# A macaron layer on one core: a fourth buffer behind the experts, chunk 3's norm moved into attention, and the prologue in another order

## The chip, the core and the metric

The kernel runs on one core of one Trainium2 chip. The core has five engines with queues of their own: PE (TensorE, matrix products), DVE (VectorE), ACT (ScalarE), POOL (GpSimd) and SP (SyncE, which only issues transfers here). They run side by side, wait for each other by semaphores, and share the on-chip memory and the eight accumulator banks that PE writes. The metric is the time of one execution on the device in microseconds (us).

## The reference

The input is x with 2 × 1024 tokens of width 128. Five steps are added to it one after the other:

```python
x = x + 0.5 * ffn0(layernorm(x))      # 16 experts, the best 4 of each token
x = x + ssm(layernorm(x))             # a convolution with powers of a, gelu, projection, layernorm
x = x + 0.5 * ffn0(layernorm(x))      # the same experts again
x = x + 0.5 * ffn1(layernorm(x))      # a dense product plus low-rank experts, the best 2 of 10
x = x + attention(layernorm(x))       # 16 heads of width 8, keys and values through a latent of 32
x = x + 0.5 * ffn1(layernorm(x))
```

An expert of ffn0 computes `glu = gate * sigmoid(1.702 * gate)`, `act = (clip(up) + 1) * glu` and `act @ down`, weighted by the token's share for that expert; the shares are a softmax over the four largest of 16 logits. In the ssm step the convolution's kernel holds the powers of a per-channel number, `a ** t` for t = 0 to 1023.

## The kernel before

The 2048 tokens are cut into four chunks of 512 (`CH`, `NC`). All float32 products are made of three products of parts: each operand is split into a high part, which the matrix unit takes in one pass, and a low part, and `split_matmul` (lines 1815 to 1817) adds high×high, low×high and high×low. So nearly every product needs two helpers: ACT copies the high part, DVE or POOL subtracts it to get the low part.

**The expert loop.** Both passes of ffn0 make one loop of `JOBS` = 128 slots (2 passes × 4 chunks × 16 experts). In a slot PE runs `expert_halves` of the slot's expert (gate and up, six products), `expert_score` in the first slots (line 1949, the shares spread over all partitions), and `expert_down` of the expert three slots earlier (lines 1966, 1967 and 1969; the last of them takes the low part). DVE runs `expert_up` (line 1344), `expert_act` of the expert before (line 1366) and `expert_weighted` (line 1355); ACT runs `expert_glu` (line 996, the gelu) and `expert_hi` (line 1010), POOL `expert_lo` (line 810). Results of these steps lie in rings: `act`, and its high and low parts in `act_parts`, have three places each (`NACT`).

Between the slots lie side chains: "in" brings a chunk in, normalizes it and makes its shares; "ssm" is the ssm step and the way to the second pass; "last" is the norm and ffn1 of chunks 0 to 2. Two tables say at which slot a step of a chain is issued on an engine: `BASE` has the slot at which a chunk's chain begins, and `STEPS` the distance of a step from it. Negative slots are the prologue, in which chunks 0 and 1 come in. `SINGLE` has the steps that occur once: `split_small` (router weights and vectors), `split0` to `split3` (the experts' weights, four experts at a time; ACT line 918 and DVE line 1331) and `powers` (lines 1319 to 1323: four small operations and a scan over 1023 elements, which the ssm step of chunk 0 needs). At each slot an engine runs its expert steps and then the side steps of that slot, in the order of the program.

**Attention.** Behind the loop, queries, keys and values of batch 0 (chunks 0 and 1) are made. Their high and low parts are put on top of each other by transfers that SP issues (`stack`, line 662), in four groups of heads; group 0 has sixteen transfers of its own, four for each of q0, k0, q1 and k1. A bound on the scores (`maxima`, line 1471, `top_norms`, `attn_bound` on PE, `root_of_bound` on POOL, `attn_spread` on PE, line 2099) gives `minus_c`, which ACT adds in the exponentials. Then 256 units run: PE makes a unit's scores (line 2111), DVE corrects those near the diagonal (`fix_scores`, line 1660), ACT takes exponentials (line 1084), and PE multiplies them into the values (line 2143). A step t of PE is two units. The tables `FIRST` and `EARLY` put other work between the units, by t for PE and by unit for DVE and ACT: what is left of ffn1 (z, weights, back), the norms and queries of batch 1, and the last ffn1 of chunks 0 to 2. Chunk 3's norm ahead of ffn1 (`LN_FFN1A`: transposes on PE, statistics on DVE, the norm on POOL, rows on ACT, transposes back at line 1863, high part at line 948, low part at line 1214) stands ahead of the first unit. The ffn1 of chunk 3 closes the program.

## Time and profile before

| | us |
|---|---|
| median of 3 runs | 710.6 (708.65 to 711.17) |
| the profiled execution, own time | 711.55 |
| its span on the core | 709.0 |
| busy: PE / ACT / DVE / POOL | 612.3 / 536.1 / 500.3 / 284.7 |

An engine's busy time is the time in which at least one of its instructions ran; its matrix products overlap, so their lengths add up to more. "Idle before" in a row is the time for which the engine had nothing to run just before that row's instructions, and the name behind the arrow is what ended most of it. The span falls into a prologue (to about 30 us), the expert loop (to about 392), attention (to about 674) and the last ffn1 of chunk 3. PE is the busiest engine in the loop and ACT in attention.

### The profile page before, as it was taken

What the parts mean: (1) busy time and instruction counts of PE and PEld (TensorE: products, weight loads), DVE (VectorE), ACT (ScalarE), POOL (GpSimd) and SP (SyncE); (2) the same over time, 40 slices, a digit from 0 to 9 for tenths busy, and PEclk for the clock granted to TensorE, in tenths of its full rate; (3) what the DMA queues carried; (4) which work ended last, traced back from release to release, by engine and by line L of the source; (5) the groups of instructions that cost most, each with busy time, mean ns of one, the idle gap of its engine ahead of it and who ended that gap; (6) DMA issues with size and microseconds to landing.
All of it is one profiled execution on the core that took longest, in us unless ns stands there. A gap on an engine that the chain in (4) does not pass through costs nothing.

```text
span 709.0 us, 11201 instructions
## 1 busy us (share of the span) xinstructions
PE 612.3 (86%) x3623; PEld 358.2 (51%) x3623; DVE 500.3 (71%) x1290; ACT 536.1 (76%) x735; POOL 284.7 (40%) x307
## 2 busy tenths in 40 slices
PE   2798898979989999999998589998987999999835
PEld 1575676657766677767676333333322333333213
DVE  3889888879988899899889634457552576555422
ACT  4566566675867857767556599999999999999911
POOL 3277557676676767555564601123310010000000
PEclk9999999999999999999999779999999999999965
DMA  9100332333333333334331699000049900000000
GB/s 263 39 1 1 125 101 90 100 79 105 91 95 100 91 95 102 104 98 127 112 98 30 147 191 244 14 0 2 1 83 196 187 13 1 1 15 16 16 3 15
DMA packets 32382, 56.64 MB, mean 80 GB/s; under 512 B 4752, under 2 KB 13424, under 8 KB 30944
## 3 DMA queue, kind: packets, MB, share of 16 engines
q1 hardware_dynamic: 31136, 55.48, 30.3%
q8 instruction: 30, 0.49, 0.3%
q0 software_dynamic: 224, 0.34, 0.2%
q14 instruction: 32, 0.26, 0.1%
q10 hardware_dynamic: 960, 0.07, 0.1%
HBM read 35.72 MB, written 3.38 MB: 55 GB/s over the span
## 4 chain that ended last, share of the span: by engine, by line
PE 30%; issue 19%; ACT 19%; DVE 15%; POOL 14%; DMA 1%; ACTq 1%; POOLq 0%; DVEq 0%
ACT raw_w L1084 13%; POOL act_parts L810 9%; PE bank L2143 8%; PE bank L1815 4%; PE bank L2111 4%; PE bank L1817 3%; DVE act L1366 3%; PE bank L1816 3%; DVE bank L1355 2%; DVE up L1344 2%; POOL rstd L757 2%; DVE stats L1204 2%; PE bank L1969 1%; DMA vecs<-in_vecs 1%; ACT L996 1%
## 5 line engine op out<-in xcount | busy, mean ns | idle before, releaser
L1084 ACT ACTIVATE raw_w<-bank,minus_c 128x1024 f32<-128x1024 f32 x256 | 260.1, 1148 | 4.1 <-PE bank L2111 3.4
L810 POOL TENSOR_TENSOR act_parts<-act,act_parts 128x512 fp32r<-128x512 f32 x128 | 167.9, 1315 | 104.3 <-ACT act_parts L1010 102.6
L1010 ACT ACTIVATE act_parts<-act 128x512 fp32r<-128x512 f32 x128 | 80.7, 631 | 97.4 <-DVE act L1366 97.1
L1660 DVE TENSOR_TENSOR bank<-bank,fix 128x256 f32<-128x256 f32 x128 | 55.5, 434 | 99.8 <-PE bank L2111 99.6
L1815 PE MATMUL bank<-xn_parts,w_hi 128*128 128x512 f32 x256 | 109.1, 426 | 13.8 <-DVE up L1344 9.9
L1344 DVE TENSOR_SCALAR up<-bank,b_up 128x512 f32<-128x512 f32 x128 | 95.3, 744 | 24.1 <-PE bank L1817 21.8
L1817 PE MATMUL bank<-xn_parts,w_hi 128*128 128x512 f32 x256 | 101.2, 395 | 0.0
L1816 PE MATMUL bank<-xn_parts,w_lo 128*128 128x512 f32 x256 | 100.8, 394 | 0.0
L1366 DVE SCALAR_TENSOR_TENSOR act<-up,bank 128x512 f32<-128x512 f32 x128 | 86.7, 677 | 0.0
L996 ACT ACTIVATE bank<-bank,b_gate 128x512 f32<-128x512 f32 x112 | 73.0, 652 | 10.4 <-PE bank L1817 10.1
L754 POOL TENSOR_SCALAR var_eps<-mean_var 128x4 f32<-128x4 f32 x28 | 6.4, 228 | 179.7 <-DVE mean_var L1535 117.0
L2143 PE MATMUL bank<-raw_w 128*9 128x512 f32 x512 | 68.4, 607 | 10.4 <-ACT raw_w L1084 9.5
L2143 PE MATMUL bank<-raw_w,act 128*9 128x512 f32 x512 | 66.9, 595 | 9.8 <-ACT raw_w L1084 9.3
L1815 PEld LDWEIGHTS bank<-xn_parts,w_hi 128*128 128x128 f32 x256 | 48.4, 189 | 36.6 <-DVE up L1344 21.2
L1969 PE MATMUL bank<-act_parts,w_hi 128*128 128x512 f32 x128 | 52.1, 407 | 9.1 <-POOL act_parts L810 9.0
L1817 PEld LDWEIGHTS bank<-xn_parts,w_hi 128*128 128x128 f32 x256 | 48.3, 189 | 11.2
L1816 PEld LDWEIGHTS bank<-xn_parts,w_lo 128*128 128x128 f32 x256 | 48.6, 190 | 7.5
L1966 PE MATMUL bank<-act_parts,w_hi 128*128 128x512 f32 x128 | 51.4, 402 | 0.0
L1967 PE MATMUL bank<-act_parts,w_lo 128*128 128x512 f32 x128 | 50.6, 395 | 0.0
L930 ACT ACTIVATE xt<-bank,offset,rstd 128x128 f32<-128x128 f32 x76 | 28.5, 461 | 13.6 <-POOL offset L763 13.6
L1355 DVE SCALAR_TENSOR_TENSOR bank<-bank,grow 128x512 f32<-128x512 f32 x48 | 33.2, 693 | 4.3 <-ACT bank L996 4.3
L1969 PEld LDWEIGHTS bank<-act_parts,w_hi 128*128 128x128 f32 x128 | 24.0, 188 | 20.9 <-POOL act_parts L810 15.7
(251 smaller groups left out, 980.1 us busy)
## 6 DMA issues: line engine op xcount, KB each, us to landing
grow<-scores SPq DMA_DIRECT2D x48, 256.0 KB, 3.2
early<-scores SPq DMA_DIRECT2D x32, 256.0 KB, 3.2
raw_w<-scores SPq DMA_DIRECT2D x32, 256.0 KB, 3.2
raw_w<-in_gate_up SPq DMA_DIRECT2D x4, 512.0 KB, 7.3
w_lo<-gelu_parts SPq DMA_DIRECT2D x8, 256.0 KB, 5.3
w_lo<-act_parts SPq DMA_DIRECT2D x8, 256.0 KB, 5.6
w_hi<-gelu_parts SPq DMA_DIRECT2D x6, 256.0 KB, 4.7
w_hi<-act_parts SPq DMA_DIRECT2D x6, 256.0 KB, 5.6
```

The lines of the kernel that those rows point to most:

```text
L810: pool.tensor_tensor(act_lo[:, j % NACT, :], act[:, j % NACT, :], act_hi[:, j % NACT, :].bitcast(F32), ALU.subtract).then_inc(s["lo_ready" ...
L996: eng.activation(out, bank[:, gate_bank(j), :], ACT.Gelu_apprx_sigmoid, bias=b_gate[:, e:e + 1]).then_inc(s["glu_ready"], 1)
L1010: eng.activation(act_hi[:, j % NACT, :], act[:, j % NACT, :], ACT.Copy).then_inc(s["hi_ready"], 1)
L1084: eng.activation(probs[:, u % NP, :], pair, ACT.Exp, bias=minus_c[:, b:b + 1])\
L1344: eng.tensor_scalar(up[:, j % 2, :], bank[:, up_bank(j), :], b_up1[:, e:e + 1], 1.0 - LIMIT, ALU.add, ALU.max).then_inc(s["up_ready"], 1)
L1366: eng.scalar_tensor_tensor(out=act[:, j % NACT, :], in0=up[:, j % 2, :], scalar=1.0 + LIMIT, in1=bank[:, weighted_bank(j), :], op0=ALU.min ...
L1660: eng.tensor_tensor(pair, pair, turned, ALU.mult).then_inc(s["fixed"], 1)
L1815: pe.matmul(out, w_hi, v_hi, start=start, stop=False)
L1816: pe.matmul(out, w_lo, v_hi, start=False, stop=False)
L1817: return pe.matmul(out, w_hi, v_lo, start=False, stop=stop)
L1969: last = pe.matmul(out, w0_hi[:, e, 2, :], act_lo[:, slot, :], start=False, stop=e == E0 - 1)
L2143: last = pe.matmul(bank[32 * j:32 * j + VW, O_BANK, :], values[b][:, kb, HG * g + j, :], probs[:, u % NP, CH * (j % 2):CH * (j % 2 + 1)], ...
```

## The change

It has three parts.

1. **A fourth buffer.** The rings of high and low parts get a place more (`NDOWN` = 4), `act` keeps three. `expert_down` now takes the expert four slots earlier, the loop runs one slot longer, `add_out` and the chains "ssm" and "last" move by one slot or stay. The memory for it comes from five small weights, which now lie in `resid`, and from `fix` and `minus_one`, which now lie in `tmp`: `fix` is loaded within the loop behind the last use of `tmp`, and POOL writes `minus_one` behind its low parts of the keys.
2. **The prologue.** Chunk 0's chain begins at slot −16 (−13 before) and the split of the small weights at −12 (−9), so that chunk 0's shares and scores stand ahead of the first weight split on DVE and of chunk 1's logits on PE. The scan of powers is cut into two halves of 511 and 512 elements, at slots −10 and −5 (one scan at slot 13 before).
3. **Chunk 3's norm inside attention.** ACT copies the transposed tokens (`keep_tokens`), DVE's statistics come behind q1's low part, POOL's norm behind the bound, and rows, high and low part are made by DVE at units 3, 5 and 6; PE transposes back at t = 2. z of chunk 2 comes ahead of that, the logits of chunk 3 behind. q1's stack transfers of group 0 come last, with a semaphore of their own that PE waits for at t = 8. DVE makes one half of k1's low part (`last_key_lo`), POOL the other, and DVE's maxima stand ahead of q1's low part.

```diff
-BASE = {"in": (-13, -12, 0, 11), "ssm": (20, 35, 51, 67), "last": (83, 99, 115)}
+BASE = {"in": (-16, -12, 0, 11), "ssm": (20, 36, 52, 68), "last": (84, 100, 116)}
...
-    "act": {"split_small": -9, "split0": -7, "split1": -3, "split2": 0, "split3": 2, "split_squares": 11, "mix0": 24, "mix1": 26, "mix2": 28},
-    "dve": {"split_small": -9, "split0": -6, "split1": -2, "powers": 13, "mix2": 29},
+    "act": {"split_small": -12, "split0": -9, "split1": -3, "split2": 0, "split3": 2, "split_squares": 11, "mix0": 24, "mix1": 26, "mix2": 28},
+    "dve": {"split_small": -12, "powers0": -10, "split0": -6, "powers1": -5, "split1": -2, "mix2": 29},
...
-    "pe": {0: ("logits", 3, 0), 1: ("logits", 3, 1), 3: ("z", 2, None), 5: ("weights", 2, None), 7: ("scores", 3, None),
+    "pe": {0: ("z", 2, None), 2: ("t2", 3, None), 3: ("logits", 3, 0), 4: ("logits", 3, 1), 5: ("weights", 2, None),
+           8: ("scores", 3, None), 9: ("back", 2, 0), 10: ("back", 2, 1), 13: ("a_t1", 2, None), 15: ("z", 3, None), 17: ("weights", 3, None),
...
-        NACT = 3
+        NACT, NDOWN = 3, 4
...
-        w_down = sb("w_down", [D, LAT])
+        w_up = resid[0:LAT, 0, 0:2 * D].rearrange("l (i d) -> l i d", i=2)
...
+            first_queries(0)
+            first_keys(0)
+            first_keys(1)
+            first_queries(1)
...
             query_lo(0)
             key_lo(0)
-            key_lo(1)
-            norm(LN_FFN1A, NC - 1)
+            key_lo(1, 0)
+
+            pool.memset(minus_one, -1.0)
...
             root_of_bound(0)
+            norm(LN_FFN1A, NC - 1)
...
+            def keep_tokens(n, c):
+                k = norm_at(n, c)
+                eng.wait_ge(s["t1_ready"], nth_t1(n, c))
+                eng.wait_ge(s["t2_ready"], k - 1)
+                eng.activation(xt[:, k % 2], bank[:, t1_bank(n, c), :].rearrange("p (t d) -> p t d", d=D), ACT.Copy)\
+                   .then_inc(s["t1_copied"], 1)
...
+            def last_key_lo():
+                c, i = QC - 1, 1
+                eng.wait_ge(s["v_ready"], c + 1)
+                eng.wait_ge(s["k_hi_ready"], 2 * c + i + 1)
+                eng.wait_ge(s["k_lo_ready"], 2 * c)
+                eng.tensor_tensor(xn_parts[:, i, chunk(c)], k_f[c][:, i, :], k_hi[:, i, place(c)].bitcast(F32),
+                                  ALU.subtract).then_inc(s["k_lo_ready"], 1)
...
-                norm_stats(LN_FFN1A, NC - 1)
-                query_lo(1)
                 maxima(0)
                 maxima(1)
                 top_norms(0)
+                last_key_lo()
                 take_bound(0)
-                norm_lo(LN_FFN1A, NC - 1)
+                query_lo(1)
+                first_stats(LN_FFN1A, NC - 1)
...
-            for slot in range(FIRST_SLOT, JOBS + 3):
+            for slot in range(FIRST_SLOT, JOBS + 4):
...
-                e, c, slot = j % E0, j // E0 % NC, j % NACT
+                e, c, slot = j % E0, j // E0 % NC, j % NDOWN
...
+                if t == KB:
+                    pe.wait_ge(s["stack0_late"], 16 * SLOTS)
...
                 keys(1)
+                norms(0)
                 values_in(1)
                 norm_in(LN_FFN1A, NC - 1, X_FFN0B)
-                norms(0)
                 norms(1)
                 pe.wait_ge(s["v_copied"], QC)
                 attn_bound(0)
-                norm_out(LN_FFN1A, NC - 1)
+                attn_spread(0)
                 pe.wait_ge(s["maxes_ready"], QC)
-                pe.wait_ge(s["xn_ready"], nth_hi(LN_FFN1A, NC - 1))
+                pe.wait_ge(s["t1_copied"], 1)
                 score_pair(0)
-                attn_spread(0)
...
-                if slot >= 3:
-                    expert_down(slot - 3)
+                if slot >= 4:
+                    expert_down(slot - 4)
```

How the rows of an engine move, at three places. First DVE in the prologue, from chunk 0's low part (L1214) on; L1228 to L1252 is the pick of a chunk, L1263 to L1299 are its shares, L1331 a weight split. Before:

```order
L1214 TENSOR_TENSOR xn_parts<-bank,xn_parts 128x512
L1228 TENSOR_TENSOR logit<-bank,router_b 128x4x16
L1233 TENSOR_TENSOR logit<-logit,bank 128x4x16
L1238 MAX top<-logit 128x8 x4
L1249 MATCH_REPLACE taken<-top,logit 128x20 x4
L1252 TENSOR_TENSOR shifted<-logit,top 128x64
L1214 TENSOR_TENSOR xn_parts<-bank,xn_parts 128x512
L1331 TENSOR_TENSOR w_lo<-raw_w,w_hi 128x1536
L1228 TENSOR_TENSOR logit<-bank,router_b 128x4x16
L1233 TENSOR_TENSOR logit<-logit,bank 128x4x16
L1238 MAX top<-logit 128x8 x4
```

After (the powers are L1320 to L1328):

```order
L1214 TENSOR_TENSOR xn_parts<-bank,xn_parts 128x512
L1320 TENSOR_SCALAR ab<-ab 128x1
L1321 RECIPROCAL ab<-ab 128x1
L1322 TENSOR_TENSOR ab<-vecs 128x1
L1323 TENSOR_SCALAR ab<-vecs 128x1
L1328 SCALAR_TENSOR_TENSOR early<-ab,zero 128x511
L1228 TENSOR_TENSOR logit<-bank,router_b 128x4x16
L1233 TENSOR_TENSOR logit<-logit,bank 128x4x16
L1238 MAX top<-logit 128x8 x4
L1249 MATCH_REPLACE taken<-top,logit 128x20 x4
L1252 TENSOR_TENSOR shifted<-logit,top 128x64
L1263 SCALAR_TENSOR_TENSOR picked<-taken,expd 128x64
```

The shares of chunk 0 stood behind the low part of chunk 1, a weight split and chunk 1's pick; now they stand directly behind its own pick, and the powers stand ahead of that pick.

Second, PE where the down projections begin: L1815 to L1817 are gate or up of an expert, L1949 its score, L1963 and L1964 the bias, L1966 to L1969 expert 0's down projection. Before:

```order
L1815 MATMUL bank<-xn_parts,w_hi 128x512 [waits up_ready]
L1816 MATMUL bank<-xn_parts,w_lo 128x512
L1817 MATMUL bank<-xn_parts,w_hi 128x512
L1949 MATMUL bank<-score_t,sel 128x512 [waits act_ready]
L1963 MATMUL bank<-score_t,db_hi 128x512 [waits score_ready]
L1964 MATMUL bank<-score_t,db_lo 128x512
L1966 MATMUL bank<-act_parts,w_hi 128x512 [waits hi_ready]
L1967 MATMUL bank<-act_parts,w_lo 128x512
L1969 MATMUL bank<-act_parts,w_hi 128x512 [waits lo_ready]
```

After (the same lines are L1827 to L1829, L1961, L1975 and L1976, and L1978 to L1981):

```order
L1827 MATMUL bank<-xn_parts,w_hi 128x512 [waits glu_ready,w0_lo_ready]
L1828 MATMUL bank<-xn_parts,w_lo 128x512
L1829 MATMUL bank<-xn_parts,w_hi 128x512
L1827 MATMUL bank<-xn_parts,w_hi 128x512 [waits up_ready]
L1828 MATMUL bank<-xn_parts,w_lo 128x512
L1829 MATMUL bank<-xn_parts,w_hi 128x512
L1961 MATMUL bank<-score_t,sel 128x512 [waits act_ready]
L1975 MATMUL bank<-score_t,db_hi 128x512 [waits score_ready]
L1976 MATMUL bank<-score_t,db_lo 128x512
L1978 MATMUL bank<-act_parts,w_hi 128x512 [waits hi_ready]
L1979 MATMUL bank<-act_parts,w_lo 128x512
L1981 MATMUL bank<-act_parts,w_hi 128x512 [waits lo_ready]
```

The down projection of an expert has moved behind the gate and up products of one more expert.

Third, PE at the start of attention: L1847 are the transposes of chunk 3, L2067 and L2068 sums of squares by head, L2094 the bound, L1863 the transposes back, L2111 the first score pair, L2099 the spread of the bound. Before:

```order
L1847 MATMUL bank<-ident,x 128x128 [waits normalized,x_ready]
L1847 MATMUL bank<-ident,x 128x128 x3
L2067 MATMUL bank<-score_t,same_head 128x512 [waits q_decayed,k_decayed,k_sq_ready,q_sq_ready]
L2068 MATMUL bank<-score_t,same_head 128x512
L2067 MATMUL bank<-score_t,same_head 128x512 [waits q_decayed,k_decayed,k_sq_ready,q_sq_ready]
L2068 MATMUL bank<-score_t,same_head 128x512
L2094 MATMUL bank<-ident,tops 1x128 [waits tops_ready,v_copied]
L1863 MATMUL bank<-ident,xt 128x128 [waits xn_ready,normalized]
L1863 MATMUL bank<-ident,xt 128x128 x3
L2111 MATMUL bank<-w_hi 128x512 [waits stack0_loaded,xn_ready,maxes_ready]
L2111 MATMUL bank<-w_hi 128x512 x3
L2099 MATMUL bank<-bound,minus_one 128x1 [waits sqrt_ready]
```

After (the transposes are L1859, the sums L2079 and L2080, the bound L2106, its spread L2111, the score pair L2123, and z of chunk 2 L1827 to L1829):

```order
L1859 MATMUL bank<-ident,x 128x128 [waits normalized,x_ready]
L1859 MATMUL bank<-ident,x 128x128 x3
L2079 MATMUL bank<-score_t,same_head 128x512 [waits q_decayed,k_decayed,k_sq_ready,q_sq_ready]
L2080 MATMUL bank<-score_t,same_head 128x512
L2106 MATMUL bank<-ident,tops 1x128 [waits tops_ready,v_copied]
L2111 MATMUL bank<-bound,tmp 128x1 [waits sqrt_ready]
L2123 MATMUL bank<-w_hi 128x512 [waits stack0_loaded,t1_copied,maxes_ready]
L2123 MATMUL bank<-w_hi 128x512 x3
L1827 MATMUL bank<-xn_parts,sq_hi 128x512 [waits z_copied,minus_c_ready]
L1828 MATMUL bank<-xn_parts,sq_lo 128x512
L1829 MATMUL bank<-xn_parts,sq_hi 128x512
```

The transposes back are gone from the place ahead of the first score pair, and the spread of the bound has come ahead of it.

## Rows read from the trace of the kernel before

**Rows 1.** Page, groups: line, operands, count; busy us, mean ns; idle before.

```profile
L1084 ACT ACTIVATE raw_w<-bank,minus_c 128x1024 f32<-128x1024 f32 x256 | 260.1, 1148 | 4.1 <-PE bank L2111 3.4
```

**Rows 2.** Waits of PE, 40 to 392 us: waiter, releaser; total us, times, longest.

```profile
PE bank L1815 <- DVE up L1344: 9.9, 16, 1.7
PE bank L1969 <- POOL act_parts L810: 9.0, 12, 1.3
```

**Rows 3.** Waits of DVE, same stretch.

```profile
DVE up L1344 <- PE bank L1817: 20.7, 26, 1.7
DVE bank L1355 <- ACT bank L996: 11.8, 8, 3.8
```

**Rows 4.** Timeline, prologue: start us, length us, engine, line, operation, [idle before, releaser].

```profile
20.63 0.22 DVE L1252 TENSOR_TENSOR shifted<-logit,top 128x64 f32<-128x64 f32 x1
...
25.13 0.22 DVE L1263 SCALAR_TENSOR_TENSOR picked<-taken,expd 128x64 f32<-128x64 f32 x1
...
21.50 0.40 PE L1879 MATMUL bank<-r_split,xn_parts 128*128 128x32 f32 x1 [1.53 <-DVE xn_parts L1214]
...
26.53 0.67 PE L1895 MATMUL bank<-ident,share_hl 128*32 128x128 f32 x4 [0.37 <-DVE share_hl L1299]
...
29.88 0.50 PE L1815 MATMUL bank<-xn_parts,w_hi 128*128 128x512 f32 x1 [0.64 <-ACT glu L996]
...
25.41 1.47 ACT L918 ACTIVATE w_hi<-raw_w 128x1536 fp32r<-128x1536 f32 x1
...
27.24 0.59 ACT L985 ACTIVATE score_t<-bank 32x512 fp32r<-32x512 f32 x1 [0.36 <-PE bank L1895]
...
27.84 1.28 ACT L996 ACT_TABLE_LOAD   x1
...
29.14 0.69 ACT L996 ACTIVATE glu<-bank,b_gate 128x512 f32<-128x512 f32 x1
```

**Rows 5.** Timeline around the powers (DVE, PE); another scan's line, min/median/max ns.

```profile
66.68 0.15 DVE L1319 TENSOR_SCALAR ab<-ab 128x1 f32<-128x1 f32 x1
...
68.01 3.16 DVE L1323 TENSOR_TENSOR_SCAN early<-ab,zero 128x1023 f32<-128x1023 f32 x1
...
71.86 0.50 PE L1815 MATMUL bank<-xn_parts,w_hi 128*128 128x512 f32 x1 [1.61 <-DVE up L1344]
...
L1394 DVE TENSOR_TENSOR_SCAN raw_w<-raw_w,zero x4: 1212/1244/1276, 106.5 to 238.5; 128x512 f32<-128x512 f32 x4
```

**Rows 6.** Timeline, start of attention: DVE, POOL, PE, ACT.

```profile
396.67 2.33 DVE L1467 TENSOR_TENSOR act_parts<-glu,gelu_parts 128x512 fp32r<-128x512 f32 x2
...
398.93 2.47 DVE L1471 TENSOR_REDUCE head_max<-bank 128x1 f32<-128x512 f32 x4
...
407.28 0.43 DVE L1660 TENSOR_TENSOR bank<-bank,fix 128x256 f32<-128x256 f32 x1 [0.97 <-PE bank L2111]
...
394.21 2.53 POOL L844 TENSOR_TENSOR xn_parts<-up,early 128x512 fp32r<-128x512 f32 x2
...
396.70 3.43 POOL L844 TENSOR_TENSOR xn_parts<-resid,early 128x512 fp32r<-128x512 f32 x2
...
406.40 0.80 PE L2111 MATMUL bank<-w_hi 32*128 32x512 f32 x4 [1.46 <-DVE xn_parts L1214]
...
407.61 1.28 ACT L1084 ACT_TABLE_LOAD   x1
```

**Rows 7.** SP's DMA issues there; table of issues: KB each, us to landing.

```profile
399.49 1.26 SPq L662 DMA_DIRECT2D w_hi<-act_parts  x2
...
402.09 1.26 SPq L662 DMA_DIRECT2D w_hi<-xn_parts  x2
...
w_hi<-xn_parts SPq DMA_DIRECT2D x4, 128.0 KB, 2.7
```

**Rows 8.** Stretches: length, busy us by engine, granted PE clock, DMA share, GB/s.

```profile
407.60:420.00 12.40, 10.87 (x65) 4.23 (x65) 4.45 (x24) 10.69 (x11) 0.00 (x0) 0.67 0.98 196
420.00:434.00 14.00, 13.00 (x102) 4.49 (x102) 5.80 (x13) 13.78 (x15) 2.78 (x2) 1.00 0.99 190
```

159 lines of the change are left out of this document (75 added, 84 removed).

## The prediction, made before the changed kernel was timed

> **What bounds the kernel now.** The profiled execution took 711.55 us, 2.55 us of it outside its span of 709.0; the median of the runs shown is 710.6, so the sum below, made against 711.55, is about 1 us high against the median. A measurement of this kernel can tell about 0.5% (3.6 us) from no change; the three chances at the end go by that.
>
> I read the page's groups first. In attention ACT is the bound: 256 exponentials of 1.148 us keep it busy for 260.1 us and only 4.1 us of idle stand ahead of them [rows 1]. So whatever lets the first exponential start earlier moves the end by as much, unless PE can't feed it. In the expert loop PE is the bound, with gaps. The waits of PE from 40 to 392 us show two large ones: 9.0 us in 12 for L1969, the third matmul of a down projection, released by POOL's low part (L810), and 9.9 us in 16 for L1815, released by DVE's `up` (L1344) [rows 2]. The waits of DVE in that stretch show that it has air, 20.7 us in 26 behind PE, and 11.8 us in 8 behind ACT's gelu [rows 3]. So a PE wait on POOL is mostly a true loss, but where ACT is the late one, removing it only moves the wait. Last I read three timelines, of the prologue, of the powers and of the start of attention; they carry the terms below.
>
> **Prologue.** Before, chunk 0's `pick` on DVE ends at 20.85 (20.63 + 0.22), but its shares start only at 25.13, behind the low part of chunk 1, the first weight split and chunk 1's pick: 4.28 us [rows 4]. Now they follow directly, so chunk 0's scores on PE move from 26.53 [rows 4] to about 22.2. That alone brings no expert forward, because two other things move back. PE's logits(1) started at 21.50; they now stand behind scores(0) and behind ACT's copy of them: 22.2 + 0.67 + 0.59 (the lengths of the two in [rows 4]) = 23.5, which is 2.0 us later. DVE's pick(1), ACT's exp(1) and ACT's second weight split behind it move with them. ACT: split 25.41 + 2.0 = 27.4, its 1.47 gives 28.9, the table load 1.28 gives 30.2 and the first gelu 0.69 gives 30.9, against 29.14 + 0.69 = 29.83 before; before, ACT had the copy of the scores between split and table load, and now has not, which is why 2.0 becomes 1.1. PE's halves(1) waited for that gelu (29.88) and will again [rows 4]. DVE's own queue grows by the powers: the four small operations and half of the scan. A 512-wide scan of another line takes 1.244 us at the median; half of the 3.16 us one would be 1.58 [rows 5]. DVE has about as much idle while it waits for logits, so this hides at the first place and adds at most 0.7 at the second. The split of small weights moves ahead of other work on ACT and DVE, but it waits for a transfer of vectors either way; I give it nothing, at most 0.4 us of gain. **+1.1 us (0 to +1.8).**
>
> **Expert loop, the fourth buffer.** PE's down(slot−3) becomes down(slot−4). POOL's low part then has one slot more, about 2.8 us (128 experts from 29.9 [rows 4] to 392, the end of the stretch of [rows 2]), and the longest wait for it was 1.3 us [rows 2]. So all 9.0 us of this wait should go. What is late next? On PE the next thing is gate and up of the following expert, which wait for DVE's `up` and ACT's gelu. DVE's waits are 20.7 behind PE against 11.8 behind ACT [rows 3]; where DVE waits behind PE a PE gain passes on, where it waits for ACT the gain is given back. So I count 20.7 / (20.7 + 11.8) = 0.64 of 9.0, that is 5.8 us. The extremes are 9.0 (all of it) and about 3 (DVE takes over at most places). The side chains move by one slot (20, 36, 52, 68 for 20, 35, 51, 67), which changes what they collide with but adds no instruction. At the end one more down projection stands behind the last halves: three matmuls, at most 3 × 0.50 = 1.5 us by the length of one in [rows 5]; I count 0.2, near the lower end, since attention waits there for other engines' work, not for PE's [rows 6].
>
> **Expert loop, the powers.** Five DVE operations between 66.68 and 71.17 (68.01 + 3.16) leave the loop, 4.4 us of DVE in one slot. PE's visible wait behind them is 1.61 us at 71.86 [rows 5]; DVE then runs the slots back to back until it has caught up, so part of the 9.9 us in [rows 2] that follows is theirs too. Between 1.6 and 4.4 I take 2.2, near the wait that is shown. The price in the prologue is counted above. **Loop together: −5.8 −2.2 +0.2 = −7.8 us (−4 to −12).**
>
> **Start of attention.** Before, PE's first score pair at 406.40 waited 1.46 us for DVE's low part of chunk 3's norm [rows 6], the end of a chain through POOL, ACT, PE, ACT and DVE. minus_c came behind that pair, then ACT loaded its table (407.61, 1.28 us) and the first exponential followed at 408.90 [rows 6]. Now the chain of the norm lies inside attention. Left ahead of the first pair are two chains. (a) The bound: the maxima (before at 398.93, after the statistics and q's low part, 2.33 us [rows 6]) start at the latest where that low part started, 396.67, and end 2.47 us later at 399.1; tops, transpose, root and spread follow. With the 1.28 us of table load behind them they may take 3.9 us before this chain and not the stacks sets the first exponential (404.3, below, less 1.28, less 399.1); before, all of that but the spread lay within the 5.0 us between the maxima's end at 401.4 and the pair at 406.40, with the norm's work in the same queues. I take it to be the earlier chain. (b) The stacks: SP issues about one DMA per 0.65 us (two in 1.26 us) and each lands 2.7 us after its issue [rows 7]. The last of group 0 was the second of the pair at 402.09; with q1's four sent last, k1's low part takes the place of the pair at 399.49, if its data are there. That data is now made by DVE (last_key_lo) at about 398.5 to 399.2. So: 399.49 + 0.63 + 2.7 = 402.8, and the first pair can run at about 403.0, 3.4 us earlier. Fix of the first pair ended at 407.28 + 0.43 = 407.71 [rows 6], 1.31 after the pair's start, so the first exponential comes at 403.0 + 1.3 = 404.3 against 408.90: −4.6. In front of the first exponentials PE now has z(2) and t2(3) in place of logits, at a granted clock of 0.67 (the level of 1.2 GHz for part of the time) [rows 8], where PE was 10.87 of 12.40 us busy; I take 0.6 back. **−4.0 us (−1.5 to −5.5).**
>
> last_key_lo is a two-input DVE operation that now stands beside POOL's same work on the other half. In the trace, POOL's two L844 took 2.53 us with DVE elsewhere and 3.43 beside DVE's L1467, whose two took 2.33 [rows 6]: about 0.45 us for each. By that row the low part is done in time for its slot in SP's queue. The Trainium skill, "SBUF — State Buffer", section "SBUF: two separate sides", says more: DVE and GpSimd share a port pair under an exclusive lock, and whichever starts first holds it for the whole instruction while the other "fully blocks". By that, one whole POOL operation would stand ahead of last_key_lo, and the term would be about −3.2 for −4.0; the rows show the partial price, and I keep to them.
>
> Attention proper is ACT's pitch, so the end moves with the first exponentials. Nothing is changed in the tail.
>
> **Sum.** +1.1 −7.8 −4.0 = −10.7: 711.55 − 10.7 = 700.85, and from the median 710.6 − 10.7 = 699.9. I predict 700.5.
>
> **Rivals.**
> R1, the low parts' wait turns into a wait for DVE's `up`: for it speaks that this wait is already the larger one [rows 2]; against it DVE's 20.7 us of waits behind PE [rows 3]. The loop then gives −3.3 for −7.8, and the time is 705.
> R2, the first pair doesn't come forward, because the last stack isn't earlier or t2 and z on one bank hold PE: attention gives −1.5 for −4.0: 703. R1 and R2 together: 707.5.
> R3, slower: the granted clock stays at 0.67 through the side chains of the first half of attention, because PE waits in order for z_copy, t_rows and hi where it had logits before. It is 0.67 until 420.0 now, after a stretch in which PE did little but wait (the last of it the 1.46 us at 406.40 [rows 6]); then 1.00, and PE is busy for 13.00 us of 14.00 [rows 8]. At half of that clock such a stretch holds 26 us of PE work in 14, so each further us at the low level costs up to 0.86 us. It decides from 12.4 us on (to about 432), when it eats the whole 10.7; with 17 us it ends at 714.5. Against it: ACT was 10.69 of 12.40 us busy in the low stretch too [rows 8], so PE fed it. The Trainium skill, page "TensorE: Matmul & The Clock Gate", section "A second HAM failure mode: psum-queue depth-cycling", reports such an oscillation from short idles between groups of matmuls; the trace shows none after 420.
> R4, the change doesn't do what it says: shares come early but no expert does. That is my forecast for the prologue already.
>
> **How the numbers follow.** Forecast 0.55 (696.5 to 704); R1 0.17 (705); R2 0.12 (703); both 0.10 (707.5); R3 0.06 (714.5). Faster by over 0.5% means below 707.0: the forecast, R1 and R2 but for some spread, 0.84; within 0.5% is R1 and R2 together and a little of the rest, 0.12; slower 0.04. The bounds of the terms added up give 694 to 707.5; with all extremes at once unlikely at the fast side, the range is 694.5 to 707.5.
>
> **What would show it.** After: no wait of PE on POOL's low part above 0.2 us in the loop, PE's wait for `up` at the old powers gone, halves(1) near 31 us, scores(0) near 22; the first exponential 4 to 5 us nearer to the loop's end, its pair released by the stack transfer; granted clock back at 1.00 within some 11 us of it. I am wrong if PE's waits for `up` grow by more than 4 us (R1), if the first pair still waits for something other than the stacks (R2), or if the low clock lasts past unit 16 (R3).

## The result and the profile after

The changed kernel took 700.41 us (median of 5 runs, 698.8 to 700.93) against 710.6 beside it (708.65 to 712.8): the ratio is 0.9843, with a 95% interval of 0.9816 to 0.987. The forecast was 700.5. The profiled execution took 698.8 us, with a span of 696.3. Two more series of the same kernel gave 0.9842 and 0.9827.

The span of a trace can be cut at four events that both kernels have: the start of the split of the small weights on ACT (which begins the routing of chunk 0), the gate product of expert 1 on PE, the loop's last add on DVE, and the first exponential. Worked out from the timelines, in us:

| | small weights start | to expert 1 | to the last add | to the first exponential | to the end of the span | span |
|---|---|---|---|---|---|---|
| before | 13.82 | 16.06 | 361.79 | 17.23 | 300.10 | 709.0 |
| after | 11.19 | 17.89 | 353.21 | 13.72 | 300.29 | 696.3 |
| difference | −2.63 | +1.83 | −8.58 | −3.51 | +0.19 | −12.7 |
| forecast | 0 | +1.1 | −7.8 | −4.6 | +0.6 | −10.7 |

**The prologue.** ACT, PE and the table of DMA issues (the last number is the time from issue to landing), to compare with [rows 4]:

```profile
11.19 0.23 ACT L903 ACTIVATE r_split<-raw_r 128x32 fp32r<-128x32 f32 x1
...
26.68 1.28 ACT L997 ACT_TABLE_LOAD   x1
27.98 0.69 ACT L997 ACTIVATE glu<-bank,b_gate 128x512 f32<-128x512 f32 x1
...
19.51 1.04 PE L1907 MATMUL bank<-ident,share_hl 128*32 128x128 f32 x4 [0.41 <-DVE share_hl L1299]
21.31 0.37 PE L1891 MATMUL bank<-r_split,xn_parts 128*128 128x32 f32 x1 [0.77 <-ACT score_t L986]
...
29.08 0.78 PE L1827 MATMUL bank<-xn_parts,w_hi 128*128 128x512 f32 x1
...
vecs<-in_vecs ACTq DMA_DIRECT2D x1, 4.0 KB, 6.3
```

Scores(0) on PE (L1907) come at 19.51 and logits(1) (L1891) behind them at 21.31, with ACT's copy between; split, table load and gelu follow in the forecast order, and expert 1 starts at 29.08 instead of 29.88. But the work from the small weights on begins 2.63 us earlier than before, since their split was not held up by the transfer of the vectors: it landed 6.3 us after its issue, 8.8 before. Counted from that start the new order is 1.83 us slower. Of that the gelu has 1.47 (16.79 us behind the start, 15.32 before). And expert 1 does not wait for the gelu any more, which ended at 28.67: its row names no wait, and the chain of work that ended last runs through DVE's second half of the powers, chunk 1's shares and PE's queue:

```profile
24.93 1.27 DVE early L1328
...
27.10 1.05 PE bank L1907 x4
```

PE was still at its lower clock there: these four products took 1.05 us where the same four took 0.60 before, and those of expert 1 are mostly 0.63 us long where they had been 0.40.

**The loop.** Waits of PE and then of DVE in the stretch of [rows 2, 3] (total us, times, longest):

```profile
PE bank L1827 <- DVE up L1345: 7.5, 14, 1.7
PE bank L1827 <- issue: 4.0, 3, 1.3
PE bank L1827 <- DVE sq_lo L1799: 2.4, 1, 2.4
```

```profile
DVE up L1345 <- PE bank L1829: 15.5, 21, 1.5
DVE bank L1356 <- ACT bank L997: 10.1, 8, 2.6
```

The wait for POOL's low part, 9.0 us in 12, is gone. The wait for DVE's `up` has not grown but fallen, from 9.9 to 7.5; it contained what the powers had cost. Two waits have grown in their place, both at the ssm step's projections: 2.4 for `sq_lo` and 4.0 in three under "issue". In the kernel before the two rows of that view for the same places are:

```profile
PE bank L1815 <- issue: 2.2, 3, 0.8
...
PE bank L1815 <- DVE sq_lo L1787: 1.2, 1, 1.2
```

DVE has less air, 15.5 us behind PE for 20.7.

One thing is new. Two stretches around the first projection, with the granted clock as the third number from the end; behind them the first of them in the kernel before, and then PE's timeline of the changed kernel at its start:

```profile
110.00:117.00 7.00, 4.89 (x17) 3.92 (x18) 5.22 (x9) 3.59 (x7) 4.05 (x4) 0.76 0.28 75
117.00:130.00 13.00, 13.00 (x60) 9.87 (x59) 12.10 (x27) 8.35 (x16) 9.36 (x10) 1.00 0.32 102
```

```profile
110.00:117.00 7.00, 5.07 (x20) 3.40 (x19) 4.31 (x8) 6.53 (x10) 5.92 (x6) 1.00 0.28 76
```

```profile
112.11 0.47 PE L1827 MATMUL bank<-gelu_parts,sq_hi 128*128 128x512 f32 x1 [2.43 <-DVE sq_lo L1799]
...
112.89 0.39 PE L1827 MATMUL bank<-xn_parts,w_hi 128*128 128x512 f32 x1
113.12 0.40 PE L1828 MATMUL bank<-xn_parts,w_lo 128*128 128x512 f32 x1
113.35 0.57 PE L1829 MATMUL bank<-xn_parts,w_hi 128*128 128x512 f32 x1
113.72 0.63 PE L1827 MATMUL bank<-xn_parts,w_hi 128*128 128x512 f32 x1
114.15 0.63 PE L1828 MATMUL bank<-xn_parts,w_lo 128*128 128x512 f32 x1
```

PE waits 2.43 us, and 1.2 us after it has started again its matmuls are 0.63 us long for 0.40, at a pitch of 0.43 for 0.23: the clock has gone from 2.4 to 1.2 GHz for some 3.4 us (0.76 over 7 us). In the trace of before all of the loop stood at 1.00; its first projection came at 116.73, behind a wait of 1.24 us.

What the fall cost can be read from two runs described below, which wait 2.44 us at the same place without a fall (the powers in the loop, and the old prologue). From DVE's `up` of slot 30 to that of slot 36, first in the changed kernel, then with the powers in the loop:

```profile
111.88 0.74 DVE L1345 TENSOR_SCALAR up<-bank,b_up 128x512 f32<-128x512 f32 x1
...
127.37 0.75 DVE L1345 TENSOR_SCALAR up<-bank,b_up 128x512 f32<-128x512 f32 x1
```

```profile
114.06 0.74 DVE L1339 TENSOR_SCALAR up<-bank,b_up 128x512 f32<-128x512 f32 x1
...
128.29 0.75 DVE L1339 TENSOR_SCALAR up<-bank,b_up 128x512 f32<-128x512 f32 x1
```

That is 15.49 us against 14.23 (14.23 with the old prologue too), so the fall costs 1.26 us.

**The start of attention.** To compare with [rows 6, 7]:

```profile
391.29 0.58 PE L2111 MATMUL bank<-bound,tmp 1*128 1x1 f32 x2 [2.10 <-POOL bound L853]
393.84 0.80 PE L2123 MATMUL bank<-w_hi 32*128 32x512 f32 x4 [1.97 <-DMA w_hi<-xn_parts]
...
391.91 0.17 ACT L1090 ACTIVATE minus_c<-bank 128x1 f32<-128x1 f32 x1 [2.61 <-PE bank L2111]
394.71 1.28 ACT L1078 ACT_TABLE_LOAD   x1 [2.63 <-PE bank L2123]
396.01 4.13 ACT L1078 ACTIVATE raw_w<-bank,minus_c 128x1024 f32<-128x1024 f32 x4
...
389.52 1.27 DVE L1466 TENSOR_TENSOR act_parts<-glu,gelu_parts 128x512 fp32r<-128x512 f32 x2
...
389.68 1.56 POOL L853 TENSOR_TENSOR bound<-bound,half_one 1x1 f32<-1x1 f32 x1 [0.96 <-DVE bound L1653]
...
390.11 1.26 SPq L651 DMA_DIRECT2D w_hi<-xn_parts  x2
```

The first score pair (L2123) waits for the stacks' transfer and nothing else, as forecast; it comes 11.55 us behind the last add (382.29) where it had been 14.73 behind it. But the table load, which I had expected to be over by then, starts only at 394.71, behind the wait for PE, and takes its 1.28 us in front of the exponential as before. The profile page's group of the exponentials is unchanged in size (259.9 us busy for 260.1, 4.9 us of idle for 4.1 in [rows 1]).

### The profile page after: what moved, and what is told of

It is laid out like the page before. It is cut to its first block, busy times and chain, and to the rows that moved or that the text cites. A ratio compares the mean times of both kernels' runs of the same rounds, so it can differ in the third digit from the quotient of the medians.

```text
span 696.3 us, 11204 instructions
## 1 busy us (share of the span) xinstructions
PE 612.3 (88%) x3623; PEld 362.0 (52%) x3623; DVE 500.7 (72%) x1297; ACT 533.0 (77%) x731; POOL 281.8 (40%) x306
## 4 chain that ended last, share of the span: by engine, by line
PE 41%; ACT 21%; DVE 20%; issue 13%; DMA 1%; POOL 1%; ACTq 1%; SPq 1%; DVEq 0%; POOLq 0%
ACT raw_w L1078 13%; PE bank L2157 8%; PE bank L1827 6%; PE bank L1829 5%; PE bank L1828 5%; DVE act L1365 5%; PE bank L2123 4%; DVE up L1345 3%; DVE bank L1356 3%; PE bank L1978 2%; PE bank L1979 2%; PE bank L1981 2%; ACT L997 2%; ACT bank L997 1%; DVE stats L1204 1%
## 5 line engine op out<-in xcount | busy, mean ns | idle before, releaser
L1078 ACT ACTIVATE raw_w<-bank,minus_c 128x1024 f32<-128x1024 f32 x256 | 259.9, 1144 | 4.9 <-PE bank L2123 4.2
L1672 DVE TENSOR_TENSOR bank<-bank,tmp 128x256 f32<-128x256 f32 x128 | 55.5, 434 | 98.3 <-PE bank L2123 98.1
L1827 PE MATMUL bank<-xn_parts,w_hi 128*128 128x512 f32 x256 | 109.9, 429 | 11.5 <-DVE up L1345 7.5
L1829 PE MATMUL bank<-xn_parts,w_hi 128*128 128x512 f32 x256 | 101.9, 398 | 0.0
L1827 PEld LDWEIGHTS bank<-xn_parts,w_hi 128*128 128x128 f32 x256 | 48.9, 191 | 35.1 <-DVE up L1345 18.4
L1829 PEld LDWEIGHTS bank<-xn_parts,w_hi 128*128 128x128 f32 x256 | 48.8, 190 | 11.2
L1978 PE MATMUL bank<-act_parts,w_hi 128*128 128x512 f32 x128 | 51.7, 404 | 0.0
L1981 PE MATMUL bank<-act_parts,w_hi 128*128 128x512 f32 x128 | 50.7, 396 | 0.0
L1356 DVE SCALAR_TENSOR_TENSOR bank<-bank,grow 128x512 f32<-128x512 f32 x48 | 33.2, 692 | 6.2 <-ACT bank L997 6.2
L931 ACT ACTIVATE xt<-bank,offset,rstd 128x128 f32<-128x128 f32 x72 | 27.0, 460 | 9.1 <-POOL offset L761 9.1
L755 POOL TENSOR_TENSOR rstd<-var_eps,half_pow 128x4 f32<-128x4 f32 x28 | 29.0, 1037 | 2.3
```

What stands on the lines that cost most here:

```text
L1078: eng.activation(probs[:, u % NP, :], pair, ACT.Exp, bias=minus_c[:, b:b + 1])\
L1827: pe.matmul(out, w_hi, v_hi, start=start, stop=False)
L1829: return pe.matmul(out, w_hi, v_lo, start=False, stop=stop)
L1978: pe.matmul(out, w0_hi[:, e, 2, :], act_hi[:, slot, :], start=False, stop=False)
```

## Experiments

All differences of stages below are between profiled executions and refer to the changed kernel's row in the table above; ratios are against the kernel before, timed beside each run.

| | ratio, 95% interval | small weights start | to expert 1 | to the last add | to the first exponential | to the end |
|---|---|---|---|---|---|---|
| three buffers | 0.9953 (0.9933 to 0.9973) | 14.21 | 17.88 | 360.31 | 13.67 | 302.43 |
| old prologue | 0.9863 (0.9817 to 0.9908) | 13.12 | 16.43 | 355.83 | 13.58 | 300.44 |
| powers in the loop | 0.9916 (0.989 to 0.9942) | 11.03 | 17.47 | 355.10 | 13.62 | 299.88 |
| old attention start | 0.9887 (0.9843 to 0.9931) | 11.06 | 17.53 | 353.38 | 17.33 | 301.10 |
| changed, again | 0.9842 (0.982 to 0.9864) | 11.04 | 17.88 | 352.97 | 13.76 | 300.15 |
| changed, third time | 0.9827 (0.9797 to 0.9857) | 11.03 | 17.88 | 353.21 | 13.71 | 301.27 |
| table load and stacks | 0.9814 (0.9788 to 0.984) | 12.29 | 17.89 | 353.11 | 11.89 | 299.52 |
| the same again | 0.9775 (0.9745 to 0.9806) | 11.79 | 17.88 | 352.97 | 11.95 | 299.71 |
| router weights first | 0.9841 (0.9817 to 0.9865) | 11.03 | 17.77 | 352.81 | 13.86 | 300.43 |
| projection later | 0.9903 (0.9873 to 0.9933) | 11.02 | 17.87 | 354.69 | 13.67 | 302.15 |
| mixed weights earlier | 0.984 (0.9811 to 0.9869) | 11.04 | 17.86 | 352.45 | 13.59 | 300.36 |
| the last and the first of these | 0.9808 (0.9767 to 0.985) | 11.31 | 17.89 | 352.45 | 11.97 | 302.68 |

### The fourth buffer taken away

```diff
-        NACT, NDOWN = 3, 4
+        NACT, NDOWN = 3, 3
...
-                if slot >= 4:
-                    expert_down(slot - 4)
+                if slot >= 3:
+                    expert_down(slot - 3)
```

> The changed kernel with the ring of parts back at three places, the down projection back at three slots behind and the chains ssm and last back at 20, 35, 51, 67 and 83, 99, 115; prologue and attention stay changed. Theory (the fourth buffer removes PE's wait for POOL's low part): PE waits for POOL in the third matmul of the down projection come back with 7 to 10 us, the last add of the loop comes 5 to 8 us later than in the changed kernel (382.3), the time is about 706 (704 to 708.5). Rival (the loop's gain is the powers' and the waits only change their name): the PE waits on POOL come back but the time is within 2 us of the changed kernel's 700.4.

708.27 us, 8.2 us above 0.9843 of the 711.28 measured beside it. PE's waits in that kernel, 40 to 392 us:

```profile
PE bank L1981 <- POOL act_parts L808: 8.7, 12, 1.2
PE bank L1827 <- DVE up L1345: 8.3, 15, 1.7
```

POOL's wait is back with 8.7 us in 12, and the loop is 7.10 us longer. The remaining 1.1 is no part of the loop in this trace, where attention took 2.1 us longer than in the changed kernel and the granted clock was once below 1.00 (0.83 over 540 to 550 us); but the profiled execution, 711.38 us, was the longest of ten, so it does not settle where the median has the 1.1. So the buffer is worth 7.1 of the loop's 8.6 us; by the 8.7 us of wait that it takes away, a share of 0.8 reached the end. The 7.1 are a net: the changed kernel loses 1.26 us to the fall of the clock at its first projection, which this run does not have, and from DVE's last `up` to the last add it took 5.4 us, as in the kernel before, for 5.9 with four buffers.

### The prologue and the powers put back

Two runs: the whole prologue as before with the powers at slot 13 (the diff, with ACT's splits back at −9 and −7 too), and the powers alone at slot 13, with chunk 0's chain and the small weights' split left at −16 and −12. The scan is one of 1023 elements again in both.

```diff
-BASE = {"in": (-16, -12, 0, 11), "ssm": (20, 36, 52, 68), "last": (84, 100, 116)}
+BASE = {"in": (-13, -12, 0, 11), "ssm": (20, 36, 52, 68), "last": (84, 100, 116)}
...
-    "dve": {"split_small": -12, "powers0": -10, "split0": -6, "powers1": -5, "split1": -2, "mix2": 29},
+    "dve": {"split_small": -9, "split0": -6, "split1": -2, "powers": 13, "mix2": 29},
```

> The changed kernel with the prologue of the kernel before: chunk 0's chain at -13, the split of the small weights at -9, the first weight split at -7 on ACT, and the powers as one scan at slot 13. Theory of the prediction (the reordered prologue costs 1.1 us and the powers out of the loop give 2.2): +1.1, about 701.5; the gate and up products of expert 1 start 1.1 us earlier than 29.1 in the changed kernel, that is near 28. Rival (the reordering itself brings the first experts forward by about 1 us, as the traces of before and after show 29.9 and 29.1): they start near 30 and the time is +3, about 703.5. Second rival (that 0.8 us is only the vectors' transfer landing earlier by chance): the start follows the landing of vecs in this run, 1.0 us per 2.6 us of landing.

> The changed kernel with only the powers moved back: one scan over 1023 elements at slot 13 in the loop, the rest of the changed prologue stays. Theory (powers in the loop cost 2.2 us, in the prologue at most 0.7): +1.5 to +2.2, about 702.3; a PE wait for DVE's up of 1 to 2 us appears near 70 us. Rival (all 4.4 us of DVE are on the path): +4. Second rival (in the prologue they cost as much as in the loop): 0.

The old prologue gave 701.44 us, near the 701.5 expected, but the interval of its ratio takes in the changed kernel's 0.9843. Counted from the small weights' start expert 1 comes after 16.43 us, 1.46 earlier than in the changed kernel, and the loop is 2.62 us longer. The row on PE's wait for `up` behind the scan:

```profile
71.58 0.79 PE L1821 MATMUL bank<-xn_parts,w_hi 128*128 128x512 f32 x1 [2.89 <-DVE up L1339]
```

The powers alone gave a prologue shorter by 0.42 and a loop longer by 1.89 us, with the same wait at the same place:

```profile
70.49 0.50 PE L1821 MATMUL bank<-xn_parts,w_hi 128*128 128x512 f32 x1 [2.87 <-DVE up L1339]
```

So by these traces the powers cost about 1.9 us in the loop and at most 0.4 in the prologue. Most of the 0.4 is the clock's: the run with the old start of attention, next, has the changed kernel's prologue with the powers in it, but expert 1's products were at the higher clock there (0.40 us long), waited 0.33 us for the gelu and came after 17.53 us, which leaves 0.06 us to the powers. The 1.9 are a net of two effects. At their own place the powers cost 3.05 us: from DVE's `up` of slot 12 to that of slot 16 it is 13.06 us with the powers alone in the loop and 10.01 in the changed kernel. Of that 1.26 are given back at the first projection, where the changed kernel's clock falls and this one's does not. The new order of shares, logits and splits costs the other 1.0 us of the prologue (1.46 less 0.42). The two runs differ by 0.73 us in the loop, and that is the clock's: both reach the `up` of slot 12 33.2 us behind expert 1, and from there to slot 16 the old prologue takes 13.77 for 13.06, with the clock down around that wait (0.66 over 70 to 75 us) in its trace alone. The old prologue's split of the small weights began when the vectors had landed, at 13.12. The run of the powers alone is odd in its times: its median, 704.02, is 4.2 us above its profiled execution (699.77, the shortest of nine), and its runs spread over 7.5 us. The two longest (707.32 and 706.85) had a mean granted clock of 0.959 and 0.961, the shortest 0.970; where they lost it the one trace doesn't show, and this stays open. By the ratio this run is 5.3 us above the changed kernel's repeat, which is nearer to the rival (all 4.4 us of DVE on the path) than to the theory's +1.5 to +2.2; against the rival speak the stages of this trace and the old prologue's run, which has the powers in the loop too and lies 1.5 us above the repeat.

### Attention's start put back

```diff
-            def first_queries(c):
+            for c in range(QC):
...
-            first_queries(0)
-            first_keys(0)
-            first_keys(1)
-            first_queries(1)
...
-                first_stats(LN_FFN1A, NC - 1)
+                norm_lo(LN_FFN1A, NC - 1)
...
-                pe.wait_ge(s["t1_copied"], 1)
+                norm_out(LN_FFN1A, NC - 1)
+                pe.wait_ge(s["xn_ready"], nth_hi(LN_FFN1A, NC - 1))
                 score_pair(0)
```

> The changed kernel with attention's start of the kernel before: chunk 3's norm ahead of the first unit, stacks in the order q0, k0, q1, k1, the maxima behind q's low part, all of k1's low part on POOL. Theory: the first exponential comes 17.2 us behind the last add of the loop again (408.90 - 391.67; 13.7 in the changed kernel) and the time rises by 3.3 to 4.0, to about 704. Rival (the norm inside attention holds PE at its lower clock and gives the gain back later): the first exponential is later by as much but the time rises by less than 1.5.

All of the third part of the change is undone here, the tables with it. 702.69 us; the ratio is 0.0045 above that of the changed kernel's repeat, which is 3.2 us. PE and ACT at the start of attention:

```profile
396.81 0.80 PE L2097 MATMUL bank<-w_hi 32*128 32x512 f32 x4 [1.46 <-DVE xn_parts L1201]
...
398.01 1.28 ACT L1071 ACT_TABLE_LOAD   x1
399.30 3.12 ACT L1071 ACTIVATE raw_w<-bank,minus_c 128x1024 f32<-128x1024 f32 x3
```

PE waits 1.46 us for the norm's low part, exactly as in [rows 6], and the first exponential is 17.33 us behind the last add: +3.61. The end moved by as much or more (attention behind it took 0.8 us longer), so nothing of the gain is given back and the lower clock is no price here.

### The transfer of the vectors

```diff
             def split_small():
-                eng.wait_ge(s["small_loaded"], 16 * len(SMALL))
+                eng.wait_ge(s["router_loaded"], 16 * 3)
...
+            def split_rest():
+                eng.wait_ge(s["small_loaded"], 16 * (len(SMALL) - 3))
```

> The changed kernel unchanged, as the control for the runs beside it. Expected 700.4 (698.5 to 703 for single runs). If the landing of the vectors' transfer, which was 10.6 to 14.2 us in the six profiles so far, sets the prologue, gate and up of expert 1 start 17.5 to 17.9 us behind the start of the small weights' split in this profile too (landing 11.2 or earlier: at 28.5 to 29.1).

> The changed kernel with the split of the small weights cut in two: the router's part waits for its own three transfers alone, the rest (down bias, vectors, up bias) follows behind chunk 0's high and low part. Theory (the landing of vecs sets when the prologue runs and gives most of the spread between runs): the router's split starts at about 11.1 us in any case, expert 1's products at 28.5 to 29.2, the median falls by about 1 us against the control and the spread of the runs shrinks from some 5 us to some 3. Rival (other transfers or the granted clock make the spread): median and spread are the control's.

> The changed kernel once more, as the control beside the run that follows: 699 to 700.5. Its profile adds one more landing of vecs (10.6 to 14.2 us so far) to the question of what sets the prologue; by the theory, expert 1's products start 17.5 to 17.9 us behind the start of the small weights' split.

The controls gave 698.95 and 699.65 us, the cut 698.93. In all fourteen profiles the small weights' split began at 11.02 to 11.19 us where the vectors had landed by then (or, in the cut, were not awaited), and otherwise within 0.1 us of their landing (11.31 to 14.21 in six); in the kernels with the powers in front expert 1 followed 17.5 to 17.9 us behind that start, early or late. So a landing behind 11.2 us moves the prologue one for one. The cut itself tells nothing: in its profile the vectors landed at 11.1, so there was nothing to win, and neither control showed the late case. That the landing differs by chance and not by the order of the kernel is likely, since the latest one (14.2, with three buffers) came with the new prologue too, but it wasn't forced.

### Where the low parts went: the projection a slot later

```diff
-           "ssm": {"t1": 0, "t2": 4, "proj": 10, "inner_t1": 11, "inner_t2": 15, "b_t1": 20, "b_t2": 24, "logits": 30, "scores": 36},
+           "ssm": {"t1": 0, "t2": 4, "proj": 11, "inner_t1": 12, "inner_t2": 16, "b_t1": 20, "b_t2": 24, "logits": 30, "scores": 36},
```

(and resid, the inner statistics, norm, rows, scale and add one slot later with it)

> The changed kernel with the ssm step's projection and what follows up to its norm (resid, inner norm, add) one slot later. In the changed kernel PE waits at the four projections for 2.43 and three times 1.33 us, 6.4 us together, where it waited 1.2 and 2.2 before. Theory (there the low part of the gelu, from POOL, is the late one, so a part of the gain of the fourth buffer is given back at these four places): the four waits fall below 2 us together and the time falls by 2 to 4 us. Rival (the waits are for something that moves along, or DVE takes over): they stay, or waits for DVE's up grow by as much, and the time is within 1 us of the control.

703.05 us, 4 above the control. The wait for `sq_lo` is gone from the list of PE's waits, 40 to 385 us, but its first row is now this, against 7.5 us in the control:

```profile
PE bank L1827 <- DVE up L1345: 14.7, 14, 2.3
```

The rival held in its mechanism: DVE, which gets the same work in a tighter place, takes over. The theory, by which the four waits would fall and the time with them, failed. The clock falls all the same (0.78 over 110 to 115 us), here behind a wait of 2.31 us for `up` at 112.31. The loop is 1.7 us longer than the control's; the rest of the 4 lies in attention (302.15 for 300.15), which this edit doesn't touch and where the clock stood at 0.66 from 530 to 540 us.

### The wait ahead of the clock's fall

```diff
-    "dve": {"split_small": -12, "powers0": -10, "split0": -6, "powers1": -5, "split1": -2, "mix2": 29},
+    "dve": {"split_small": -12, "powers0": -10, "split0": -6, "powers1": -5, "split1": -2, "mix2": 28},
```

> The changed kernel with DVE's part of the mixed weights (sq_lo, line 1799) at slot 28 for 29. In the changed kernel its data are there at 105.8 us, but it stands behind a weighting that waits until 110.9 for ACT's gelu; PE waits 2.43 us for it at 112.1, and then runs at the granted clock of 0.5 for some 4 us (0.72 to 0.84 in 110 to 115). Theory (the long wait brings the clock down, both are one cost of about 3 us): PE's wait at that place falls to about 1.3 us, as at the other three projections, no stretch below 1.00 is left between 30 and 385 us, and the time falls by 2 to 3 us against the control's 699. Rival (DVE's queue is the late one whatever stands in it, as moving the projection showed): the wait for DVE moves to the next slot and the time is within 1 us of the control.

700.04 us. PE's row at the first projection, POOL's low part of the gelu, and the stretch around them:

```profile
111.09 0.47 PE L1827 MATMUL bank<-gelu_parts,sq_hi 128*128 128x512 f32 x1 [1.91 <-issue]
...
109.72 1.27 POOL L781 TENSOR_TENSOR gelu_parts<-glu_s,gelu_parts 128x512 fp32r<-128x512 f32 x1
...
110.00:117.00 7.00, 5.91 (x21) 4.76 (x22) 5.87 (x12) 3.51 (x7) 4.13 (x4) 0.76 0.22 75
```

The wait for `sq_lo` is gone, but 1.91 us remain (under "issue", as at the other projections), the clock still falls to 0.76 over the same 7 us, and the loop is shorter by 0.5 us only. My theory fell: the late operand there is another one. Gelu's low part from POOL is the one left; it ends at 110.99, 0.10 us ahead of PE's start, but no run moved it. The fall of the clock couldn't be taken away at this place either.

### The table load and the stacks: a faster version

```diff
-        minus_c = sb("minus_c", [128, NB])
+        minus_c = sb("minus_c", [128, NB + 1])
...
-            first_queries(0)
-            first_keys(0)
-            first_keys(1)
-            first_queries(1)
+            for part, c in (("q_hi", 0), ("k_hi", 0), ("q_lo", 0), ("k_lo", 0), ("k_hi", 1), ("k_lo", 1),
+                            ("q_hi", 1), ("q_lo", 1)):
+                first(part, c)
...
+                eng.activation(minus_c[:, 2:3], minus_c[:, 0:1], ACT.Exp)
```

> The changed kernel with two edits at the start of attention: one tiny exponential behind minus_c, so that ACT loads its table while PE waits, and k0's high part sent ahead of q0's low part by SP, which stood idle for 1.2 us there. Theory (the stacks' transfers release the first score pair, then fix and the 1.28 us table load stand in a row ahead of the first exponential): the pair comes 1.2 us earlier and the exponential 2.1 to 2.5 us nearer to the loop's last add (13.7 before, 11.3 to 11.6 now), the time falls by about 2.2, to about 698.2. Rival (PE is at its lower clock there, and what ACT wins it waits for later): the first exponential is as early but the end moves by less than 1 us.

> The version with the table load ahead and k0's high part ahead of q0's low part, once more beside the control, since 697.7 against 699.0 left open whether it is faster. Theory (the first exponential is 1.85 us nearer to the loop's last add, and attention behind it as long as before): 1.3 to 2.0 us below the control. Rival (the difference was the spread of the runs): within 0.7 us of the control.

> The edit of v7 together with the two at the start of attention (table load ahead, k0's high part ahead of q0's low part). Theory: the gains add, 699 - 2.5 - 1.9 = 694.6, against 697.7 with the attention edits alone. Rival: the gain of v7 is not there, 697.5.

697.69 and 695.73 us, against controls of 698.95 and 699.65 beside them: 1.3 and 3.9 us less, and a ratio of 0.9775 to 0.9814 against the kernel before. It is the fastest kernel of the study. The first pair of runs alone would leave that open, since their single times overlap; with both, and the stage table, it holds. ACT, DVE, PE and SP:

```profile
392.90 0.17 ACT L1091 ACTIVATE minus_c<-bank 128x1 f32<-128x1 f32 x1 [2.61 <-PE bank L2113]
393.09 1.28 ACT L1111 ACT_TABLE_LOAD   x1
395.18 2.12 ACT L1079 ACTIVATE raw_w<-bank,minus_c 128x1024 f32<-128x1024 f32 x2 [0.59 <-PE bank L2125]
...
395.22 0.43 DVE L1674 TENSOR_TENSOR bank<-bank,tmp 128x256 f32<-128x256 f32 x1 [2.23 <-PE bank L2125]
...
394.35 0.80 PE L2125 MATMUL bank<-w_hi 32*128 32x512 f32 x4 [1.48 <-DMA w_hi<-xn_parts]
...
386.01 1.26 SPq L651 DMA_DIRECT2D w_hi<-act_parts  x2
388.38 1.26 SPq L651 DMA_DIRECT2D w_hi<-xn_parts  x2
```

The table is loaded at 393.09, while PE waits, and the first exponential follows the score pair directly, 0.83 us behind its start (2.17 in the changed kernel), and 11.89 us behind the last add for 13.76 in the control. It does not wait for fix (L1674), which ran only from 395.22. The stacks gave less than the 1.2 us I had expected: the pair comes 11.06 behind the last add for 11.59, since SP now stands idle for 1.1 us one place later (387.27 to 388.38), where k0's low part isn't made yet. The 3.9 us of the second run are more than the 1.3 to 2.0 expected, and the traces put 1.8 of it at the first exponential and 1.5 behind that, where the edit changes nothing, less 0.5 ahead of it. Why attention was shorter stays open; the four runs below 696.1 us had a mean granted clock of 0.972 to 0.974, the profiled one (697.46) 0.967. With the mixed weights' edit added, 698.88 us and a ratio that can't be told from it, where the two gains added would have given 694.6; in that trace the clock fell in attention too, around a wait of PE for the exponentials, and attention is 3 us longer:

```profile
530.20 1.90 PE L2159 MATMUL bank<-raw_w,act 128*9 128x512 f32 x8 [2.29 <-ACT raw_w L1079]
...
525.00:540.00 15.00, 12.02 (x85) 3.74 (x80) 3.58 (x9) 11.73 (x13) 0.00 (x0) 0.77 0.97 194
```

## Why the prediction was right

Its total was right, and for the most part for its own reasons. Three of its steps failed and two were off in size; that the errors of the stages nearly cancel (+0.7 in the prologue, −0.8 in the loop, +1.1 at the start of attention, −0.4 behind it) is luck. Also, 2.6 us of the profiled execution's gain came from when a transfer landed.

- **Prologue, +1.1 (0 to +1.8): near the upper end, and by another path.** Counted from the small weights' start +1.83 here, +1.46 against the old prologue in the changed kernel, of which 0.42 lie between the changed kernel and the run with the powers in the loop (in the old prologue's run scores(0) on PE took 1.03 us for 0.67 before, which makes the 0.37 between the two numbers). At the gelu, against the old prologue, it is +1.10 (16.79 for 15.69). The step with the scores ahead of logits(1) holds: moved back by the 2.63 us, scores(0) stand at 22.1 and expert 1 at 31.7, for 22 and 31. But that expert 1 would wait for the gelu again failed: PE's queue, at the lower clock behind the shares, brought it 0.4 us behind the gelu's end. Two of the twelve runs with the new order, the powers in the loop and the old start of attention, show such a wait (0.35 and 0.33 us), and in both PE was at the higher clock by then. The other step that failed is the one on the transfer, "at most 0.4 us of gain": it landed 2.6 us earlier in this execution, and expert 1 came 0.8 us early instead of 1.1 late. In the chain of waits of the kernel before that transfer stood with 1% of the span; what one trace can't show is that its landing moves by 3.7 us between executions.
- **Fourth buffer, −5.8: right in kind, too small.** The wait of 9.0 us disappeared, and 7.1 us of it reached the end. My factor of 0.64, from the ratio of DVE's waits, should have been 0.8, and its reason did not show: DVE's wait for ACT did not grow (10.1 us, 11.8 before). What was lost went into the fall of the clock, 1.26 us, and the longer end of the loop, 0.6 where I had counted 0.2. PE's waits at the projections grew by 3.0 us; how much of that is a loss beside these two was not separated.
- **Powers, −2.2: right as a net** (1.9 and 2.6 in the two runs), and that partly by luck. At their place they cost 3.05 us; 1.26 of it is lost again in the fall of the clock, which came in all ten profiles with the powers in front and four buffers, and in the 2.6 a fall of its own counts 0.7. The prediction had neither.
- **Start of attention, −4.0: right in its chain, −3.3 in size.** The stacks release the first pair and it came 3.2 us nearer to the last add (forecast 3.4). The step that failed is the one from the pair to the first exponential, 1.3 us by the end of fix, with the table load hidden: it took 2.17. ACT loads the table only behind the wait that stands ahead of the exponential, so its 1.28 us stayed in the chain, and the first exponential does not wait for fix at all. The version with a tiny exponential ahead shows both: there the load is hidden and the step takes 0.83. In return the 0.6 us to be given back were 0.2.
- **Rivals.** R1 did not happen here (waits for `up` fell to 7.5) but did with the projection a slot later (14.7): DVE is that close. R2 did not happen: the pair came 3.2 us nearer. R3 did not happen at the start of attention, where the clock was back at 1.00 some 8 us behind the first exponential; its mechanism, a wait of PE and then a fall of the clock, showed elsewhere, at 113 us, for 1.26 us.
- **The Trainium skill's rule on the port.** The section "SBUF: two separate sides" of "SBUF — State Buffer" could not be seen at last_key_lo, which met no POOL work. It could be seen beside it: the root on POOL (L853, one element) took 1.56 us, from 389.68, while DVE's L1466 ran (two from 389.52 to 390.79, in the rows of the start of attention above). In the kernel before, with no such work of DVE beside it, the same operation is:

```profile
402.70 0.57 POOL L854 TENSOR_TENSOR bound<-bound,half_one 1x1 f32<-1x1 f32 x1 [0.46 <-DVE bound L1641]
```

The operation took 1.56 us in all twelve profiles with this order and 0.57 in the two with the old one. That agrees with one engine blocking the other for whole instructions. It delayed minus_c, not the first pair. The prediction had read a partial price of 0.45 us out of POOL's L844 beside DVE's L1467 [rows 6], and that reading was wrong. The single operations there (shortest, median and longest in ns, first and last start) are:

```profile
L1467 DVE TENSOR_TENSOR act_parts<-glu,gelu_parts x2: 660/1206/1751, 396.7 to 397.2; 128x512 fp32r<-128x512 f32 x2
...
L844 POOL TENSOR_TENSOR xn_parts<-resid,early x2: 1706/1732/1759, 396.7 to 398.4; 128x512 fp32r<-128x512 f32 x2
```

DVE's first operation started first and took 0.66 us; its second took 1.75, and POOL's two 1.76 and 1.71 for 1.29 alone. Each of these three is longer by nearly what the other engine's running operation still had to go (1.1 for 1.2 us at DVE's, 0.5 and 0.4 for 0.6 each at POOL's), so these rows agree with the rule of whole instructions too.

Without the 2.63 us of the transfer the stages add up to −10.1 (+1.83 −8.58 −3.51 +0.19), and 710.6 less 10.1 is 700.5, where 700.41 was measured. So over many executions the transfer seems to be worth little, as it would be if its landing goes by chance; with one profiled execution of the kernel before, that is argued and not shown.

## What to carry to other kernels

One more place in a ring took a wait away here, where the engine behind it (POOL, busy for 40% of the span) had air; read that engine's own waits first, and then look at the clock and at the next points where PE waits, since part of the gain was lost there and not where I looked. Put one dummy operation of the next activation table behind the last use of the old one, where the engine then waits anyway. Compare two traces only from the first event that does not hang on a transfer, since its landing may move everything behind it.
